# Sixty-four free bytes ahead of the expert part's buffers, in an attention and mixture-of-experts kernel

## What is computed

```python
q = softmax(x @ Wq, axis=-1);  k = softmax(x @ Wk, axis=-2);  v = x @ Wv
ctx = einsum('bnd,bne->bde', k, v) * scale
x = layernorm(x + (q @ ctx / D_OUT) @ Wo + bo)

vals, idx = top_k(x @ wr.T, 2);  gating = softmax over the two
xg = x_pad[dispatch]                              # rows gathered for each expert
h = gelu(einsum('ecd,edf->ecf', xg, w1) + b1)     # 256 -> 1024
y = einsum('ecf,efd->ecd', h, w2) + b2            # 1024 -> 256
out = layernorm(x + segment_sum(y * g))
```

## Time and profile before

| | |
|---|---|
| median of three runs | 2108.64 us (2108.2 to 2109.53) |
| the profiled execution | 2106.24 us, span 2104.2 us |
| TensorE, matmuls and weight loads | 2019.2 us (96%) and 1966.2 us (93%) |
| VectorE, ScalarE, GpSimd | 1454.5, 1235.8 and 1249.0 us (69%, 59%, 59%) |
| chain that ended last | TensorE 62% of the span, no other engine over 3% |

### The profile page before, as it was taken

The page is one execution under the profiler, slowest core; times in us unless marked ns, Lnnn a source line. Parts: engine busy times, 40 slices in busy tenths (PEclk is TensorE's granted clock), DMA queues, the critical chain, the costliest instruction groups (busy, mean ns, idle before and its releaser), DMA issues.

```text
span 2104.2 us, 51595 instructions
## 1 busy us (share of the span) xinstructions
PE 2019.2 (96%) x16208; PEld 1966.2 (93%) x16209; DVE 1454.5 (69%) x4361; ACT 1235.8 (59%) x2770; POOL 1249.0 (59%) x1321
## 2 busy tenths in 40 slices
PE   6999999998869999999999999999999999999996
PEld 5988888887869999999999999999999999999996
DVE  3877877886757676667668666766776676666665
ACT  3566666665635656565656565656565655556553
POOL 1377777777846565556555555555566555555564
PEclk9999999999879999999999999999999999999998
DMA  5244344333132112112112211121131121121221
GB/s 189 86 139 149 116 134 149 119 126 112 62 123 83 42 46 87 50 43 91 50 50 76 70 54 58 52 96 56 60 99 64 56 65 62 64 64 63 70 70 48
DMA packets 102241, 173.30 MB, mean 82 GB/s; under 512 B 26179, under 2 KB 70430, under 8 KB 102064
## 3 DMA queue, kind: packets, MB, share of 16 engines
q0 software_dynamic: 45104, 84.59, 12.7%
q1 hardware_dynamic: 57088, 88.18, 12.4%
HBM read 120.52 MB, written 68.97 MB: 90 GB/s over the span
## 4 chain that ended last, share of the span: by engine, by line
PE 62%; issue 3%; DMA 2%; POOL 2%; DVE 1%; DVEq 1%; ACT 0%; POOLq 0%; ACTq 0%
PE y_ps L1676 30%; PE h_ps L1660 29%; PE tb_ps L1641 3%; DMA rows<-x_rows,pick_idx 1%; POOL rows L1389 1%; DMA out<-y,put_idx 1%; POOL base L1402 0%; POOL rstd_b L1395 0%; POOL out L1413 0%; ACT h_ps L1481 0%; DVE y_raw L1527 0%; POOLq L1427 0%; DVEq L1344 0%; DVE h_lo L1593 0%; DVE y L1560 0%
## 5 line engine op out<-in xcount | busy, mean ns | idle before, releaser
L1481 ACT ACTIVATE h_ps<-h_ps,b_sb 128x256 f32<-128x256 f32 x1000 | 404.0, 446 | 573.4 <-PE h_ps L1660 573.4
L1676 PE MATMUL y_ps<-w_hi,h_hi 128*128 128x256 f32 x2000 | 571.2, 286 | 5.1 <-DVE h_lo L1593 5.0
L1660 PE MATMUL h_ps<-bt_hi,w_hi 128*128 128x256 f32 x2000 | 559.4, 280 | 2.7 <-DVE bt_lo L1509 1.4
L1676 PE MATMUL y_ps<-w_lo,h_hi 128*128 128x256 f32 x2000 | 559.8, 280 | 0.0
L1676 PE MATMUL y_ps<-w_hi,h_lo 128*128 128x256 f32 x2000 | 559.5, 280 | 0.0
L1660 PE MATMUL h_ps<-bt_lo,w_hi 128*128 128x256 f32 x2000 | 558.4, 279 | 0.0
L1660 PE MATMUL h_ps<-bt_hi,w_lo 128*128 128x256 f32 x2000 | 558.2, 279 | 0.0
L1593 DVE TENSOR_TENSOR h_lo<-h_ps,h_hi 128x512 fp32r<-128x512 f32 x500 | 336.5, 684 | 72.9 <-ACT h_hi L1484 71.8
L1676 PEld LDWEIGHTS y_ps<-w_hi,h_hi 128*128 128x128 f32 x2000 | 378.0, 189 | 6.5 <-DVE h_lo L1593 6.4
L1660 PEld LDWEIGHTS h_ps<-bt_hi,w_hi 128*128 128x128 f32 x2000 | 376.7, 188 | 4.4 <-issue 2.5
L1676 PEld LDWEIGHTS y_ps<-w_hi,h_lo 128*128 128x128 f32 x2000 | 377.3, 189 | 0.0
(11 more groups left out here) (279 smaller groups left out, 3600.8 us busy)
## 6 DMA issues: line engine op xcount, KB each, us to landing
xt_raw<-in_x_t SPq DMA_DIRECT2D x32, 512.0 KB
x_raw<-in_x SPq DMA_DIRECT2D x64, 256.0 KB, 3.2
w_raw<-in_w SPq DMA_DIRECT2D x16, 1024.0 KB
x_rows<-x_sb SPq DMA_DIRECT2D x32, 512.0 KB
out<-alone SPq DMA_DIRECT2D x32, 512.0 KB, 4.6
slot_table<-entry,where POOLq DMA_INDIRECT x256
out<-y,put_idx POOLq DMA_INDIRECT x253
rows<-x_rows,pick_idx POOLq DMA_INDIRECT x250, 2.8
```

Of the source, the lines that this page charges most:

```text
L1481: nc.scalar.activation(half, half, ACT.Gelu_apprx_tanh, bias=b1_sb[:, bass.ds(e * FT + 2 * g + i, 1)]).then_inc(gelu_done, 1)
L1660: ins = nc.tensor.matmul(h_ps[:, g, (f % 2) * BLK:(f % 2 + 1) * BLK], w[:, c:c + P], v[:, k, :], start=(i == 0), stop=(i == 3 * DK - 1))
L1676: ins = nc.tensor.matmul(y_ps[:, t, :], v[:, g, h:h + P], w[:, c:c + D], start=(f == 0 and t == 0 and part == 0), stop=(f == FT - 1 and t ...
```

## The change

Sixteen float32 a partition, 64 bytes, are declared ahead of all other buffers of the expert part and used by nothing. So every buffer of that part moves 64 bytes up. The attention part and the kept buffers stay where they are. No instruction is added, removed or moved.

```diff
@@ -1299,6 +1299,8 @@
             def ps(name, shape):
                 return phase.enter_context(nc.psum_tensor(name, shape, F))
 
+
+            sb("ahead", [P, 16])
             w_hi[1] = sb("w_hi1", [P, 2 * DK * FF], R)
             w_lo[1] = sb("w_lo1", [P, 2 * DK * FF], R)
             TCOLS = E * EC
```

## The result

The changed kernel is slower: 2115.38 us, the median of eight runs (2113.47 to 2117.7), against 2108.42 us for eight runs of the kernel before. The ratio is 1.0036, with a 95% interval of 1.0027 to 1.0044. The forecast was 2089.4, and 2084 to 2102 for the range. The profiled execution took 2115.96 us, with a span of 2114.0.

What follows compares the result with a forecast made beforehand. TensorE's matmul pace in the expert part was taken as the bound. Undisturbed even blocks 15.2, splitting stretches 3.1 and odd-to-even blocks 0.9 sum to 19.2 us, so 2108.64 falls to 2089.4 us; range 2084.8 to 2093.9, or 2084 to 2102 with partly caught.

Steps and rivals of the forecast that it cites:

- Odd experts keep every distance among weights, x^T and h: The other 45 undisturbed blocks of odd experts: no distance changes, so nothing gained or lost.
- other engines: VectorE, ScalarE, GpSimd and transfers in the expert part: nothing taken, between -0.5 and +0.5 us in all.
- Undisturbed even blocks: 35 blocks of even experts fall from 11.827 to 11.393 us each, 15.2 us saved, all on the path.
- only part is caught: Rival, even experts: up alone or down(1) to down(3) alone gets fast, gain 11 or 8 us, 2098.3 or 2100.7; 16%.
- In the odd experts up and down have opposite signs, and both are fast: Argument against the partly caught rival: offsets modulo 256 of either sign allow the fast pace in odd experts.
- The splitting stretches of even experts: Five blocks per even expert holding the splitting and the weight load: 0.8 us saved each, 3.1 us in all.
- The blocks from odd to even: First even block after each odd expert, three of them: 0.3 us saved each, 0.9 us in all.
- the other way: The block on the way back from even to odd experts, 11.86 us: it won't move.
- No change: Rival: even experts are slow for another reason belonging to the first set of weights; time stays 2108.6 us; 8%.
- slower: the weights' own place: Rival: weights' own place modulo 128 decides, odd experts fall to the even pace, 21.8 us lost, 2130.4 us; 8%.

Runs made afterwards that it cites:

- the rows put right: The changed kernel with the gathered rows also moved by 64 bytes, all else behind them by 256, against the kernel before: 2094.31 us, ratio 0.9941.
- the first and third group: Sets of pad or stand-in kernels, each group run on one chip beside the kernel before, which took 2106.94 us in the first and 2107.7 us in the third.

## Why the prediction was wrong

The reading of the kernel before was right: TensorE's pace bounds it, the pace depends on how its operands lie to each other, and absolute places don't matter. The first set moved alone gives 2085.9 on a chip where before takes 2106.9: 21.0 us, for the forecast 19.2. What failed are two statements on what the change does to the distances.

**"Odd experts keep every distance among weights, x^T and h", so nothing.** True as written, and the wrong list. The run behind the transposes is where the fast pace is caught, I had said so, and the last thing that TensorE loads ahead of it is `rows`, a kept buffer that stays behind when h moves. At 192 the run is caught, at 128 it was slow in every undisturbed block of the changed kernel. In the profiles the 33 undisturbed blocks of experts 1, 3 and 5 went from 376.0 to 386.3 us, 10.3 more, and the last twelve intervals of expert 7 cost another 3.6, 13.9 us in all where the sum had 0. The trace before couldn't price this, but the declarations showed it, and the text names `rows` only for its transfer. What I ruled out for "other engines" I never asked for TensorE's own fourth operand.

**Undisturbed even blocks, 15.2 us.** They gave 413.95 - 408.66 = 5.3 (46.74 + 104.97 + 93.48 + 163.47 = 408.66). With the rows put right they take 11.541 us, a gain of 35 x (11.827 - 11.541) = 10.0, so the rows hold 4.7 of the missing 9.9; the other 5.2 are the side. I had counted modulo 128 because only 64 and 0 seemed to differ; the kernels show that 128 is not the period; moves by 256, such as that of the first set against x^T and h where the rows alone were moved, left the blocks as they were (11.83 in even ones). The rival "only part is caught" named the other side, with 16%, and priced it at 8 to 11 us of gain; the kernel with the rows put right lies a little above that (2106.94 - 2094.31 = 12.6), though not by its mechanism: up and down get fast and slow in whole blocks by turns, and neither of them for good. "In the odd experts up and down have opposite signs, and both are fast" was the false argument against it: turned round, the same pair doesn't hold the pace from block to block. Each share is read from one kernel, and the side cost more in the kernel whose first set moved by 192, 11.75 in all of expert 4.

**The smaller terms.** The splitting stretches of even experts gave 1.7 for 3.1 (239.85 to 238.11 us), within their bounds, and those of experts 1, 3 and 5 lost 1.3. The blocks from odd to even gave 1.4 for 0.9, just over the bound of 1.3; the other way lost 0.9. The first of line 1612 came 2.3 us later in the profiled execution (636.05 for 633.71), which can't be put down to the change: in the kernels of the first and third group it came anywhere from 633.9 to 636.9, without a trend. In sum 2.3 - 5.3 + 10.3 + 3.6 - 1.7 + 1.3 - 1.4 + 0.9 = 10.0 us, beside 9.8 us of span; the medians of runs differ by 7.0.

**The rivals.** "No change" and "slower: the weights' own place" have both fallen, the second by the kernel in which everything moved. The sign that it gave was right for another reason: it too had odd experts losing their pace. None of my cases held a loss by the source of the transposes, and so the 8% for slower stood for a mechanism that these runs rule out. The Trainium skill ("SBUF — State Buffer", "Who interferes with whom") gives TensorE two independent read ports. The trace doesn't bear out what the rival drew from that, a pace that no address changes: at one granted clock, 1.00, the same 100 instructions take 11.34 to 11.95 us by the place of the buffers alone.

Open is what happens inside. No row shows a read, and that a load of the stationary operand and a stream of the moving one meet is inferred from the pitch. Why 128 is the bad distance for the transposes' source and 192 the good one for the weights, and why the pace changes where it does, I can't derive.

## What to carry over

When TensorE is the bound and its matmuls come back to back, measure their pitch by stretch. If equal code runs at two pitches, list the place of every operand that TensorE reads there, those of the transposes in between too, modulo 256 bytes (as far as the steps tried here tell), and copy all distances of the fast stretch, not the one that seems to matter. Padding one buffer so that it keeps the others where they are, as with the first set of weights here, touches fewer pairs than a pad ahead of everything. A stretch that a change "doesn't touch" is safe only if nothing that its bounding engine reads moves against anything else that it reads.

## What the runs showed of the hardware

- With weights at 192 or 64, a run of matmuls with 256 columns has two steady paces, 113.3 to 113.8 and some 117.8 ns, and keeps one of them for dozens of matmuls. It changes within the first matmuls of a new kind: behind the transposes, but also from up to down(0) (5.44 us for 48, then 1.42 for 12) and from down(3) to up (in the changed kernel 4.25 for 36, then 5.46 for 48; with its rows moved 4.09, then 5.66). With weights at 0 and 128 no undisturbed block had the fast pace; a matmul took 120 ns at 0 and 118.5 to 118.9 at 128.
- The pace depends on distances between operands, not with a period of 128 bytes, and not on absolute addresses: 64 bytes ahead of everything left the windows of 106.45 and 148.11 us as they were.
- With weights at 192, the place of the source of four transposes decides in nearly every undisturbed block the pace of the 84 matmuls behind them (36 and 48), worth 0.31 us of an 11.4 us block, without any change in the transposes themselves: 0.44 us for the four in blocks of 11.34 us and of 11.75.
